# Trainium2: factors of the attention's norm turned by one product and read back repeated over the channels, in a cross-attention and sparse-FFN kernel

## The reference

```python
def xattn(q, k, v, Wq, Wk, Wv, Wo, bo, g):          # b=32, c=64, n=512
    qh = einsum('bcn,oc->bon', q, Wq).reshape(b, 8, 64, -1)
    kh, vh = (the same of k with Wk, of v with Wv)
    qh = softmax(qh, axis=-2) * SCALE
    kh = softmax(kh, axis=-1)
    context = einsum('bhdn,bhen->bhde', kh, vh)
    out = einsum('bhde,bhdn->bhen', context, qh).reshape(b, 512, -1)
    out = einsum('bcn,oc->bon', out, Wo) + bo[None, :, None]
    norm = maximum(sqrt(sum(out * out, axis=1, keepdims=True)), 1e-12)   # over the 64 channels
    return out / norm * g * sqrt(64)
def ffn(x, c1_w, c2_w, w1, w2t):                    # rows of 512
    blk = (xf @ c1_w.T @ c2_w.T).reshape(rows, 56, 32)
    idx = argmax(blk, axis=-1) + arange(0, 1792, 32)
    h = relu(einsum('bkm,bm->bk', w1[idx], xf))
    return einsum('bk,bkm->bm', h, w2t[idx])
x = x + xattn(layernorm(x), ctx, ctx, ...)          # layernorm over the 512 tokens
x = x + ffn(layernorm(x), ...)
```

## Time and profile before

| | |
|---|---|
| time, 3 runs | 764.76, 764.79, 768.7 us, median 764.79 |
| profiled execution | 764.77 us, of it span 762.7 |
| PE, DVE, ACT, POOL busy | 739.2, 624.0, 402.3, 486.9 us |
| granted TensorE clock, mean | 0.991 |
| attention steps | from the start to about 397 us |
| seam and FFN | from about 397 us on, 8 duos |

### The profile page before, as it was taken

The page is one execution under the profiler, slowest core; times in us unless marked ns, Lnnn a source line. Parts: engine busy times, 40 slices in busy tenths (PEclk is TensorE's granted clock), DMA queues, the critical chain, the costliest instruction groups (busy, mean ns, idle before and its releaser), DMA issues.

```text
span 762.7 us, 14646 instructions
## 1 busy us (share of the span) xinstructions
PE 739.2 (97%) x5210; PEld 565.2 (74%) x5210; DVE 624.0 (82%) x910; ACT 402.3 (53%) x773; POOL 486.9 (64%) x549
## 2 busy tenths in 40 slices
PE   8989999999999999999995999999999999999998
PEld 6555665665665666665664989989898998989896
DVE  7978999999999999999956778787777878777652
ACT  5879999999999999998831112102111110211010
POOL 3899999998888888677554363463536346363420
PEclk9999999999999999999997999999999999999999
DMA  6244334333333333221201203022130311211011
GB/s 166 63 113 118 104 102 130 97 105 104 98 81 97 94 83 97 70 72 56 76 18 26 78 20 105 21 52 76 24 102 21 104 21 49 78 22 49 20 53 34
DMA packets 66376, 55.23 MB, mean 72 GB/s; under 512 B 40704, under 2 KB 49536, under 8 KB 66304
## 3 DMA queue, kind: packets, MB, share of 16 engines
q1 hardware_dynamic: 65648, 53.57, 25.8%
q10 hardware_dynamic: 656, 0.72, 0.3%
HBM read 38.52 MB, written 8.39 MB: 62 GB/s over the span
## 4 chain that ended last, share of the span: by engine, by line
PE 71%; POOL 17%; DVE 4%; issue 3%; ACT 2%; SPq 2%; DMA 1%; DVEq 0%; POOLq 0%; ACTq 0%
PE slot L1113 20%; PE po L1131 10%; PE turn L1131 10%; PE po L1243 7%; POOL Q L534 7%; PE turn L1228 5%; PE slot L1269 4%; PE turn L1211 4%; PE slot L1283 3%; POOL weights_lo L483 3%; POOL c_low L516 2%; POOL x_low L473 2%; SPq L275 2%; PE slot L1095 2%; PE po L1254 1%
## 5 line engine op out<-in xcount | busy, mean ns | idle before, releaser
L534 POOL TENSOR_TENSOR Q<-Q,qrec 128x1024 f32<-128x1024 f32 x64 | 121.4, 1905 | 36.3 <-DVE qrec L775 36.3
L422 POOL TENSOR_TENSOR E<-E,rank 128x512 bf16<-128x512 bf16 (+1 forms) x64 | 71.1, 1111 | 108.6 <-DVE E L624 107.6
L1246 PE MATMUL po<-QT,G 128*64 128x512 f32 x256 | 116.9, 599 | 0.0
L1243 PE MATMUL po<-E,ctxT 128*64 128x512 f32 x256 | 116.9, 599 | 0.0
L945 ACT ACTIVATE E<-slot,neg_kmax 128x512 f32<-128x512 f32 x128 | 86.3, 686 | 8.8 <-DVE neg_kmax L761 8.5
L435 POOL TENSOR_TENSOR behind<-E,first 128x512 bf16<-128x512 bf16 (+1 forms) x64 | 60.4, 944 | 41.9 <-DVE first L632 41.7
L727 DVE TENSOR_REDUCE qmax<-slot 128x16 f32<-128x1024 f32 x64 | 75.3, 1217 | 12.6 <-PE slot L1283 12.6
L1243 PEld LDWEIGHTS po<-E,ctxT 128*64 128x64 f32 x256 | 32.3, 136 | 65.4 <-issue 58.5
L761 DVE TENSOR_REDUCE neg_kmax<-slot 128x2 f32<-128x1024 f32 x64 | 76.4, 1194 | 3.8 <-PE slot L1269 2.9
L767 DVE TENSOR_REDUCE qsum<-Q 128x16 f32<-128x1024 f32 x64 | 77.3, 1208 | 2.2 <-ACT Q L934 1.5
L953 ACT ACTIVATE E<-turn 128x512 f32<-128x512 f32 x128 | 74.8, 612 | 3.7 <-PE turn L1211 2.7
(11 more groups left out here) (185 smaller groups left out, 1970.0 us busy)
## 6 DMA issues: line engine op xcount, KB each, us to landing
c_in<-in_ctx SPq DMA_DIRECT2D x64, 128.0 KB, 2.6
x_in<-in_x SPq DMA_DIRECT2D x64, 128.0 KB, 2.6
stage<-in_ffn_w SPq DMA_DIRECT2D x32, 225.0 KB, 2.6
attn_out<-po_sb SPq DMA_DIRECT2D x32, 128.0 KB, 2.3
out<-E SPq DMA_DIRECT2D x16, 256.0 KB, 2.3
ctxT<-in_ctxT SPq DMA_DIRECT2D x31, 128.0 KB, 2.5
attn<-attn_out SPq DMA_DIRECT2D x9, 256.0 KB, 3.6
E<-attn_out SPq DMA_DIRECT2D x7, 256.0 KB, 4.0
```

The source lines that it names most:

```text
L534: nc.gpsimd.tensor_tensor(half, half, qrec[1 - par][:, s, :].unsqueeze(2).broadcast_to([P, HALF, D]), ALU.mult).then_inc(q_scaled, 1)
L1243: nc.tensor.matmul(po[0:C, :], ctxT[1 - par][:, m, :], E[1 - par][:, :, m * P:(m + 1) * P], start=(m == 0), stop=(m == NT - 1)).then_inc(p ...
L1246: nc.tensor.matmul(po[C:P, :], G[:, m, :], QT[m][:], start=(m == 0), stop=(m == HT - 1)).then_inc(out_mm, 1)
```

## The change

In a steady duo the tile isn't multiplied while it is turned. ACT squares the turned tile in its PSUM bank, DVE sums it, POOL raises the factors of both tiles in one instruction (`invert(a, 2)`, 128x16), PE turns these 128x16 into 16x128 (`turn_factors`), and ACT copies the 16 rows, stores them to a DRAM tensor `factors` and loads each tile's factors back so that a row of 512 tokens stands in all 64 partitions of its batch (`exchange`). Then the unturned tile is multiplied with it (`scale`), and nothing is turned back. `turn_attn`, the squares and the norms of tiles a + 2 and a + 3 move into the end of the duo before. For tiles 0 and 1 the factors are stored as they are, 4 bytes at a time (`store_factor`), and POOL scales. Their steps are `TURNS` = 24 and 27. The items of the weights start at step 4 with pairs in 14 steps, the last batch's result is stored from ACT's queue, the seam and the duos have a new order. `gate`, `first_max`, `select` and the rest are called in another order too.

```diff
-FIRST_ITEMS, PAIRS = 2, 12
+FIRST_ITEMS, PAIRS = 4, 14
+TURNS = (B - 8, B - 5)
...
+        over_channels = lambda a: factors[a].unsqueeze(1).broadcast_to([2, C, N])
+        by_token = lambda f: f.rearrange("b (t p) -> p (b t)", p=P)
+        turned_inv = pre[0][0:4 * NT, 0:P]
...
+                def store_factor(a):
+                    sp.wait_ge(norm_inv, a + 1)
+                    sp.dma_start(by_token(factors[a]), inv[:, a], allow_slow_non_contiguous=True).then_inc(first_stored, 16)
+
+                def load_factor(a):
+                    sp.wait_ge(first_stored, 16 * (a + 1))
+                    sp.dma_start(spread_of(a), over_channels(a)).then_inc(spread_in[a], 16)
...
-                    nc.scalar.activation(work_of(a), bank[:], ACT.Square).then_inc(squared, 1)
...
+                    nc.scalar.activation(bank[:], bank[:], ACT.Square).then_inc(squared, 1)
+
+                def exchange(d):
+                    a = 2 * d + 2
+                    act.wait_ge(inv_turned, d + 1)
+                    if d:
+                        act.wait_ge(factors_stored, 16 * d)
+                    nc.scalar.activation(inv_rows[:], turned_inv, ACT.Copy).then_inc(rows_kept, 1)
+                    act.wait_ge(rows_kept, d + 1)
+                    nc.scalar.dma_start(factors[a:a + 2].rearrange("a b (t n) -> (a b t) n", n=P), inv_rows[:])\
+                        .then_inc(factors_stored, 16)
+                    act.wait_ge(factors_stored, 16 * (d + 1))
+                    act.wait_ge(scaled, a)
+                    for t in range(2):
+                        nc.scalar.dma_start(spread_of(a + t), over_channels(a + t)).then_inc(spread_in[t], 16)
...
+                        if known == B + 1:
+                            act.wait_ge(po_copied, g)
+                            nc.scalar.dma_start(scratch[g - 2], po_sb[par][C:P, :]).then_inc(stored[par], 16)
...
                 def duo(d, last_duo):
                     a = 2 * d + 2
-                    if not last_duo:
-                        turn_attn(a, pre[0])
-                        turn_attn(a + 1, pre[1])
                     if d:
                         down(d - 1, 5)
+                    if not last_duo:
+                        turn_factors(d)
                     hide(d, 1)
                     if d:
                         down(d - 1, 6)
-                    else:
-                        project(d, 5)
                     project(d, 6)
                     hide(d, 2)
-                    if not last_duo:
-                        turn_back(a, pre[0])
-                        turn_back(a + 1, pre[1])
                     down(d, 0)
                     project(d, 7)
                     down(d, 1)
...
                     down(d, 3)
+                    if d + 2 < DUOS:
+                        turn_attn(a + 2, pre[0])
+                        turn_attn(a + 3, pre[1])
                     if not last_duo:
                         project(d + 1, 4)
                         hide(d + 1, 0)
```

More of the change, by code:

```diff
@@ L78, in real, with program @@
     return known is None or 0 <= known + shift < B
-def program(nc, A, scratch, out):
+def program(nc, A, scratch, factors, out):
     with ExitStack() as ctx:
@@ L659, in duo @@
                     h_low(d, 0)
-                    if not last:
-                        norms(a)
                     first_max(d, 4)
                     block_max(d, 5)
-                    if not last:
-                        norms(a + 1)
-                        scale(a)
                     first_max(d, 5)
@@ L671, in duo @@
                     gate(d, 1)
-                    if not last:
-                        scale(a + 1)
                     block_max(d, 6)
                     h_low(d, 1)
+                    gate(d, 2)
                     if not last:
-                        residual(a, pre[0])
-                    gate(d, 2)
+                        for t in range(2):
+                            scale(a + t)
+                            residual(a + t)
+                            moments_of(a + t)
+                        normalize(a)
                     first_max(d, 6)
                     if not last:
-                        residual(a + 1, pre[1])
-                    h_low(d, 2)
+                        normalize(a + 1)
                     block_max(d, 7)
-                    if not last:
-                        normalize(a)
-                        normalize(a + 1)
-                    first_max(d, 7)
                     if not last:
@@ L695, in duo @@
                         z_low(d + 1)
-                    h_low(d, 4)
+                    h_low(d, 3)
                     if not last:
@@ L844, in _ @@
                 block_max(0, 4)
+                norms(2, pre[0])
+                norms(3, pre[1])
                 gate(0, 0)
@@ L1056, in turn_attn, with turn_factors @@
                     last.then_inc(attn_turned, 1)
-                def turn_back(a, bank):
-                    pe.wait_ge(scaled, a + 1)
-                    if a < 2:
-                        pe.wait_ge(q_copied, HT * (B - 5 + a) + 4)
-                    for t in range(NT):
-                        last = nc.tensor.transpose(bank[:, t * P:(t + 1) * P], turned_of(a)[:, t * P:(t + 1) * P], ident[:])
-                    last.then_inc(attn_back, 1)
+                def turn_factors(d):
+                    pe.wait_ge(norm_inv, inverted(2 * d + 2))
+                    nc.tensor.transpose(turned_inv, inv[:].rearrange("p a f -> p (a f)"), ident[:]).then_inc(inv_turned, 1)
                 def turn_x(a, bank):
@@ L1292, in step @@
                         pe.wait_ge(rest_in, 32)
-                    if known in (B - 3, B - 2):
-                        turn_back(known - (B - 3), turn[(8 * g + 1) % 3])
+                    if known in TURNS:
+                        turn_attn(TURNS.index(known), turn[(8 * g) % 3])
+                    if known in (B - 2, B - 1):
+                        turn_x(known - (B - 2), turn[(8 * g) % 3])
                     for m in range(HT):
@@ L1333, in build @@
     scratch = nc.dram_tensor("attn_out", (B, C, N), fp32, kind="Internal").ap()
-    program(nc, A, scratch, out)
+    factors = nc.dram_tensor("factors", (TILES, 2, N), fp32, kind="Internal").ap()
+    program(nc, A, scratch, factors, out)
 def kernel(x, ctx_4096, L0_xattn_Wq, L0_xattn_Wk, L0_xattn_Wv, L0_xattn_Wo, L0_xattn_bo, L0_xattn_g,
```

231 lines of the change are left out of this document (117 added, 114 removed).

## The result

The changed kernel takes 823.42 us, median of 4 runs (819.74 to 830.12), against 766.75 for the kernel before on the same chip: a ratio of 1.0749, 95% interval 1.067 to 1.0829. Slower, as forecast, but by more than the range allowed. The profiled execution took 819.74, its span 818.1, 55.4 more than before.

| stretch | before | after | difference | forecast |
|---|---|---|---|---|
| start to step 24 | 285.42 | 282.55 | -2.9 | -3.9 |
| step 24 to step 31 | 85.36 | 108.66 | +23.3 | +11.4 |
| step 31 to first turn_x | 55.68 | 56.74 | +1.1 | -1.3 |
| six duos | 267.89 | 299.01 | +31.1 | +30 |
| from the last turn_x on | 68.3 | 71.1 | +2.8 | 0 |

The account below looks back on a forecast made before the run. PE was taken to bound the FFN, POOL and then DVE the attention. Early attention -3.9, six duos +30, seam -1.3 and attention's tail +11.4 gave +36.2 on the 762.7 span, 798.9, so 801 us; range 758 to 814.

Parts of the forecast that it names:

- The price between 3.6 and 14.5 us: Duo's two 256 KB factor loads: quick landing 3.6 us, or two engines only, 8.5 and 14.5; the latter chosen, chance 0.72.
- F + 17.6: Duo: second tile's factors arrive 17.6 us after turn_factors starts (F): 3.1 to the small store's end, 14.5 for loads.
- the line's 2.9: POOL's 128x16 power in a duo: 2.9 us by the line through 128x1 and 128x8, bounds 1.65 and 3.3.
- from P to turn_factors: Duo: from the start of project(d+1, 4), turn_factors can start after 10.25 us; PE arrives at 8.9, so stands 1.4.
- x + 5.6 + 8.5 = x + 14.1: Attention's tail, step 25: load_factor(0) lands 14.1 us after DVE's step start (x), 8.5 of it for landing.
- Its own sign of being wrong: Small factor stores: a landing above 5 us was listed among what would show the forecast wrong.
- The second rival: Attention's tail: 4-byte stores add 5 us in steps 25 and 28, loads quick; about 770 us; chance 0.08.
- the forecast of 403: Seam: the factors' chain begins near 403 us, so turn_x(3) can start at 425.3; -1.3 us.
- Early attention: Weight items from step 4, not 2: 5.0 us saved at step 4, less 1.1; -3.9 us, bounds -2 and -5.
- four more steps at POOL's pace: Attention: pair steps 4 to 17 instead of 4 to 13, four more at 0.28 us each, costing 1.1 us.
- The first rival: Factor loads: all 16 engines share each load by its 128 destination partitions; -5.1 us, time 759.7; chance 0.20.
- the 1.39 that was feared: DVE's new scale and residual: contention with POOL could make each 1.39 instead of 0.73 us, 4 us over six duos.

## Why the prediction was right and wrong

**Right: the sign and the duo.** The price between 3.6 and 14.5 us was taken at the high end, and it is there: landings of 7.9 and 13.8 us after the first issue, forecast 8.5 and 14.5. The small store took 1.3 us and not 2.3, so the second tile's factors came at F + 16.1 and not F + 17.6, and turn_x at F + 21.0 in the seam and 20.6 in a duo, not 22.3. The power of 128x16 took 3.35 us, above the line's 2.9 and at its upper bound, and PE stood 1.75 us and not 1.4: from P to turn_factors it took 10.9 us, not 10.25 (614.29 to 625.17). Together a duo of 48.5 us in place of 49.6, which is +23.4 for six. That they still cost 31.1, as the 30 forecast, is luck, a second error that went the other way: three duos took 49.0 to 52.2 us from one turn_factors to the next. In the one from 475.94 to 528.17 the granted clock was 0.89 from 497 on, behind waits of 2.00 and 1.34 us, and the turns of the second tile took 1.11 us, not 0.66; behind 0.95 and 1.34, in the duo from 576.62 on, it stayed at 1.00. Behind 1.94 and 1.34, in the first duo, it stayed there too, so these rows give no length of wait at which it falls. The forecast had no term for the clock, which took some 6 us of the six duos (an estimate, from its mean of 0.98) and 2.8 of the stretch behind them. With the waits before turn_x gone the period is 45.8 in each duo, at the full clock.

**Wrong: the tail, +23.3 and not +11.4.** The step that failed is the one that reads "It lands at x + 5.6 + 8.5 = x + 14.1", with its premise under the rivals: "nothing waits for the store until the load behind the scratch store, 5 us later". The store was given no time of its own beyond that. Its own sign of being wrong, "a landing of the small stores above 5 us", names this term. The store takes 11.9 us from its issue to the load behind it, the load is issued at x + 13.2 and scale begins at x + 20.5. The second rival had this store, but with 16-engine loads, "5 us in each", and at 0.08; it and the forecast were not alternatives. Both hold, and the sum needed both: the split store took 15.3 us out of the stretch and the split load 8.9, and with both it is 87.86 against 85.36 before. DVE waited 11.3 us for x at the statistics of step 26 and 13.2 at those of step 29; the forecast had 4.8 us for the first and, at residual(1), 9.1 for the second. With +11.4 in this place the time would have been some 811.5, inside the range.

**Wrong in size: the seam, +1.1 and not -1.3.** SyncE was freed as forecast: the masks' transposes start 19.9 us behind step 31 (411.07), 7.1 sooner than before. But the factors' chain begins at 426.91, 35.7 us behind step 31, and the forecast of 403 was 32.2 behind it. PE stood 8.1 us for the power, which stood behind a select that waited 4.9 us for DVE's first maximum:

```profile
422.47 1.04 POOL L467 TENSOR_TENSOR behind<-E,first 128x512 bf16<-128x512 bf16 x1 [4.92 <-DVE first L658]
423.47 3.38 POOL L426 TENSOR_TENSOR inv<-norm,neg_half 128x16 f32<-128x16 f32 x1
...
426.91 0.38 PE L1090 MATMUL turn<-ident,inv 128*16 128x128 f32 x1 [8.10 <-POOL inv L426]
```

Moving that maximum gave 2.9 us in the seam. The forecast didn't follow POOL's list through the seam.

**Early attention, -2.9 and not -3.9.** Step 4 starts at 53.95, as forecast (53.7). The sum counted four more steps at POOL's pace, 1.1 us. The pair steps 4 to 7 had not been at that pace before, and six more were (6 to 17 for 8 to 13). Alone the edit gives 3.2 us.

**The first rival**, 16-engine loads with a time of 759.7, had the price of its condition wrong as well: a version with such loads and the short store takes 768.34. With 1.75 us at turn_factors in each duo and 8 us in the seam its gain is gone.

## What to carry to other kernels

Look at the leading dimension of both sides of a DMA before costing it: a broadcast that begins with 2 runs on two engines and also holds up whatever is issued behind it, and two loads that begin with 64 cost only one more issue. Where an edit adds several transfers in a chain, give each its own landing time: stores in pieces of 4 bytes have one that no row of 2 KB pieces shows, and let nothing that waits for such a store stand ahead of the next batch's work. A step later on POOL took POOL's wait away; SyncE, which met the load right behind the store all the same, still stood. Rivals that are independent of each other belong in one sum; kept apart as cases, they leave out the case in which both are true.

## What was not expected of the hardware

A store of 4 KB in 1024 pieces of 4 bytes took 11.9 us from issue to the next instruction that waited for it (295.72 to 307.62); 128 pieces of 32 bytes landed in 2.2. A load of x took 8.2 us behind a load on two engines, 3.4 behind the same bytes loaded with 64 in front. The power on POOL took 1.68 us for 8 columns and 3.35 for 16, twice as much, while 1 column took 0.55. The scale with two inputs in SBUF took 0.69 us in ten of its fourteen uses, not the 1.39 that was feared, and 0.94 to 0.97 in the four in which a product on POOL ran beside it.
